# One core, third layer: where the gelus of a sequence stand, and who places the activation-table loads

## The reference, cut to what matters

```python
# attention branch: two "forgetting" attentions (forward and backward), 16 heads
f = jax.nn.log_sigmoid(xn @ Wf.T + bf)        # abs, exp and log on ACT
probs = softmax(scores + cumulated gates)     # exp on ACT
o @ Wo.T
# feed-forward branch: two small transformer layers (DEPTH = 2)
for l in range(2):
    ...local attention over windows of 64, 8 heads, softmax (exp on ACT)
    h = (h - mu) / sqrt(var + 1e-05) * lg + lb
    h = h @ w1 + b1
    a, g = jnp.split(h, 2, axis=-1)
    h = a * jax.nn.gelu(g, approximate=False)  # gelu on ACT
    x = x + h @ w2 + b2
```

## Time and profile before

| | |
|---|---|
| time, median of 3 runs | 2943.32 us (2940.13 to 2945.33) |
| profiled execution: span, first to last instruction | 2847.3 us |
| median of the runs less that span | 96.0 us |
| third layer within the span | about 665 to 2243 us |
| mean granted TensorE clock over the span | 0.954 |

### The profile page before, as it was taken

The page is one execution under the profiler, slowest core; times in us unless marked ns, Lnnn a source line. Parts: engine busy times, 40 slices in busy tenths (PEclk is TensorE's granted clock), DMA queues, the critical chain, the costliest instruction groups (busy, mean ns, idle before and its releaser), DMA issues. The chain is left out here.

```text
span 2847.3 us, 76648 instructions
## 1 busy us (share of the span) xinstructions
PE 2442.7 (86%) x30232; PEld 1812.5 (64%) x30232; DVE 2005.6 (70%) x5914; ACT 1823.8 (64%) x3779; POOL 787.6 (28%) x820
## 2 busy tenths in 40 slices
PE   6858999996889999999999899989996658999964
PEld 6745677774556666566656665666664547999943
DVE  5556544444568776877687677877775498999988
ACT  3334555553566666666666667666763488999997
POOL 3325100002133232323232223222222163111167
PEclk9959999997999999999999999999999689999998
DMA  6201355551000000000000000000000014666611
GB/s 211 38 16 40 115 158 160 155 156 56 11 17 15 4 17 17 15 4 17 17 15 4 17 17 17 9 10 13 14 13 7 1 45 156 203 195 202 192 42 51
DMA packets 104306, 175.17 MB, mean 62 GB/s; under 512 B 16273, under 2 KB 73745, under 8 KB 103825
## 3 DMA queue, kind: packets, MB, share of 16 engines
q1 hardware_dynamic: 94608, 153.20, 18.0%
q0 software_dynamic: 8192, 16.79, 2.0%
q10 hardware_dynamic: 1152, 0.27, 0.0%
HBM read 130.50 MB, written 26.74 MB: 55 GB/s over the span
## 5 line engine op out<-in xcount | busy, mean ns | idle before, releaser
L2014 POOL TENSOR_TENSOR l_rinv<-l_ssm,w_neg_half 128x8 f32<-128x8 f32 x128 | 210.2, 1642 | 551.8 <-DVE l_ssm L2305 551.7
L257 PE MATMUL bank<-l_kT,l_qT 32*128 32x128 f32 (+1 forms) x3072 | 355.0, 350 | 8.8 <-DVE l_qm L1382 7.2
L257 PE MATMUL bank<-l_qm,l_kT 32*128 32x128 f32 (+1 forms) x3072 | 350.7, 347 | 6.3 <-DVE l_qm L2215 6.3
L2045 ACT ACTIVATE l_probsT<-bank 128x768 f32<-128x768 f32 x256 | 208.5, 815 | 160.1 <-PE bank L257 159.3
L276 DVE TENSOR_REDUCE l_tops<-bank 128x2 f32<-128x256 f32 (+1 forms) x384 | 196.1, 511 | 119.9 <-PE bank L257 116.5
L2717 DVE RECIPROCAL l_rden<-l_den 128x256 f32<-128x256 f32 x128 | 223.8, 1748 | 30.0 <-ACT l_den L2628 29.4
L893 POOL DMA_INDIRECT back<-sorted_y,pos x128 | 125.6, 981 | 378.7 <-DMA sorted_y<-l_y_tile 347.8
L277 DVE TENSOR_REDUCE l_tops<-bank 128x2 f32<-128x512 f32 (+1 forms) x384 | 227.5, 592 | 0.0
L257 PEld LDWEIGHTS bank<-l_kT,l_qT 32*128 32x128 f32 x3072 | 205.8, 190 | 18.2 <-DVE l_qm L1382 9.3
L257 PEld LDWEIGHTS bank<-l_qm,l_kT 32*128 32x128 f32 x3072 | 202.9, 188 | 8.2 <-DVE l_qm L2215 8.1
L154 POOL TENSOR_TENSOR l_rstd<-l_var,w_neg_half 128x2 f32<-128x2 f32 (+1 forms) x56 | 42.6, 760 | 569.6 <-DVE l_var L149 556.8
(11 more groups left out here) (350 smaller groups left out, 6967.4 us busy)
## 6 DMA issues: line engine op xcount, KB each, us to landing
l_expert<-in_experts SPq DMA_DIRECT2D x72, 768.0 KB, 4.1
l_expert<-in_experts SPq DMA_DIRECT2D x72, 578.0 KB, 3.5
l_x_tile<-sorted_x SPq DMA_DIRECT2D x144, 64.0 KB, 4.1
sorted_y<-l_y_tile SPq DMA_DIRECT2D x144, 64.0 KB, 3.7
l_v_half<-l_v SPq DMA_DIRECT2D x32, 264.0 KB, 3.2
sorted_x<-x_all SPq DMA_DIRECT2D x18, 256.0 KB, 3.9
l_v_half<-l_v SPq DMA_DIRECT2D x32, 132.0 KB, 3.2
l_x<-in_x SPq DMA_DIRECT2D x8, 256.0 KB, 5.0
```

Source lines behind the costliest of these rows:

```text
L257: lasts.append(pe.matmul(bank[:, at:at + n * P], lhs[:, c * P:(c + 1) * P], rhs[:, x0 * P:(x0 + n) * P], start=False, stop=(i == 1), skip_ ...
L2014: pool.tensor_tensor(rinv[:, i, :], ssm[:, i, :], g.neg_half[:, 0:LH], ALU.pow).then_inc(rinv_ready[l], 1)
L2045: Bt.took(act.activation(probsT[:, (j // 2) % 2, 2 * (j % 2):2 * (j % 2) + 2, :], two[:, :, 0:AW], ACT.Exp), rd, use)
```

## The change

The three `up` items of each small layer now stand at one step (5 for small layer 0, 8 for small layer 1), and the source places the table loads: `natural_log_exp_and_others` once at the start of the third layer on ACT, `gelu_and_others` ahead of a small layer's first gelu, and `natural_log_exp_and_others` again behind its third. The order within the steps changes on every engine, since all walk `BESIDE`. No DMA is added, removed or moved.

```diff
-    3: [("o", 1, 0), ("o", 1, 1), ("qk", 0, 1), ("up", 0, 0)],
+    3: [("o", 1, 0), ("o", 1, 1), ("qk", 0, 1)],
     4: [("qk", 0, 2), ("out", 1)],
-    5: [("up", 0, 1), ("up", 0, 2)],
+    5: [("up", 0, 0), ("up", 0, 1), ("up", 0, 2)],
     6: [("shift", 1), ("down", 0), ("apply", 1)],
     7: [("normed", 1), ("qk", 0, 3)],
-    8: [("qk_t", 0, 0), ("up", 1, 0), ("up", 1, 1)],
-    9: [("up", 1, 2), ("qk_t", 0, 1)],
+    8: [("qk_t", 0, 0), ("up", 1, 0), ("up", 1, 1), ("up", 1, 2)],
+    9: [("qk_t", 0, 1)],
     10: [("down", 1), ("qk_t", 0, 2), ("hand", 1)],
...
             act.wait_ge(setup_done, 1)
+            act.preload_act_table_set("natural_log_exp_and_others")
...
                         l, m = of
+                        if m == 0:
+                            act.preload_act_table_set("gelu_and_others")
                         b = G.read(act, rd, item)
                         act.activation(gg[:, m, :], b[:, S:2 * S], ACT.Gelu,
                                        bias=w["bup2"][:, l, 1, m:m + 1]).then_inc(gelu_ready[l], 1)
+                        if m == FC - 1:
+                            act.preload_act_table_set("natural_log_exp_and_others")
```

## The result

The changed kernel takes 2917.7 us (median of 4 runs, 2913.7 to 2919.9) against 2941.7 (2938.3 to 2945.3): ratio 0.9921, 95% interval 0.9907 to 0.9936. (Ratios stand here as they were recorded with the runs; they are not exactly the quotients of the medians.) It is 24 us faster; the forecast was 15 us slower, and the time lies under both ranges, 2946 to 2970 and 2930 to 2975.

What follows compares the result with a forecast made beforehand. No engine is full; DVE sets the pace in steps 3 to 14, ACT in 16 to 18. Step 5 +16.5, steps 8 and 9 +17.5, gates -18.0, ends -1.5: +14.5 us, 2957.8 us; range 2946 to 2970, 8 in 10 2930 to 2975.

Steps and rivals of the forecast that it cites:

- What lies around the span, 96.0 us against the median of the runs, stays: Whole kernel: 96.0 us of run time outside the profiled span of 2847.3 us was taken as unaffected by the change.
- The gates: Steps 16 to 18: log and exp share a set, two loads go; 1.2 us gained a round, bounds 0.64 and 2.57.
- Step 5: Small layer 0: the third `up` waits for a bank, so DVE is 1.1 us late a round; bounds 0 and 1.9.
- The chain of 2.34: Step 5: gelu, DVE multiply, PE's pairs, gelu; 2.34 us from first gelu to third at full clock.
- Step 8: Steps 8 and 9, small layer 1: the third `up` waits for DVE; 1.25 us lost a round, bounds 0 and 1.5.
- three small differences of terms near 1 us decide: Warning on the round's sum, 1.1 + 1.25 - 1.2: if the gates give over 2.3, the kernel is not slower.
- What a load costs: ACT's table loads: the trace shows 1.30 us from load to next instruction, the Trainium skill about 2.66 for a switch.
- Faster: the batch pays: Rival, 14%: the third `up`'s bank wait is hidden at steps 5 and 8, the gates' gain stands; -19.5 us, 2924 us.
- No change: Rival, 18%: gates give 2.57 a round, or the losses at steps 5 and 8 are half as large; 2937 or 2941 us.
- Slower still: Rival, 12%: gates give only the first two waits and PE's 1.5 us carries in full; 2970 or 2982 us.
- the build would place loads of its own: Rival, 2%: the build adds its loads beside the source's, 65 more on ACT; about 2995 us.

Runs made afterwards that it cites:

- quick chip: Kind of chip (1 and 15) on which the unchanged kernel before takes 2852 to 2854 us; the changed kernel's ratio there is 1.0006.
- late profiles: Profiles on the kind of chip (14, 10, 0) where the kernel before takes 2943 to 2947 us; the changed kernel's ratios there are 0.9908 and 0.9921.
- chip 14: One of three chips where the unchanged kernel before takes 2943 to 2947 us; its profiled round there is 96.17 us.

## Why the prediction was wrong

**The step that failed** is "What lies around the span, 96.0 us against the median of the runs, stays". I took the trace for the runs' own execution. It was not: 1.7 to 3.2 us lie around a span, and the 93 us that remained were lost inside the kernel, on the kind of chip that was timed. Some of them could be won by the change. The sum had no term for PE's late signals and none for the clock, since the trace that it was read from showed neither. The table of a round makes the sum. The late signal is the rounds at full clock (94.65 before, 94.30 after) less the quick chip's; the falls are what is left of the mean over 13 rounds. The changed kernel has two late profiles:

| us a round | before | changed | difference |
|---|---|---|---|
| quick chip | 93.4 | 93.8 | +0.4 |
| late signal at step 19 | +1.2 | +0.5 | -0.7 |
| clock falls | +1.5 | +0.1, +0.35 | -1.4, -1.2 |
| late chip, mean | 96.17 | 94.42, 94.64 | -1.75, -1.53 |

Thirteen rounds give -20 to -23 us of the -24 measured. On chip 14, from the gates of the first sequence to those of the last, the kernel before took 1405.0 us and the changed one 1382.3: -22.7, nearly all in these 13 rounds. In the result's own profile the same stretch took 1380.4; there the two rounds ahead of the 13 were 4.7 us shorter as well, and differences of that size in these two rounds come and go between late profiles.

**Terms.** The gates: forecast -1.2, measured -1.47, within the bounds of 0.64 and 2.57. Step 5: forecast +1.1, measured +0.67. The chain of 2.34 was right (2.35), but on the quick kind the first gelu came 1.26 earlier in the round and not 0.8, so the last product was 0.70 late. Step 8: forecast +1.25, measured +1.03 on the late kind and 1.09 on the quick one, with the wait of 1.5 as worked out. In sum +0.34 in place of +1.15: three errors of 0.2 to 0.4, all on one side. On the quick kind the forecast's +14.5 us on the span was +5.4 (2847.7 to 2853.1), and the ratio says no change. So even there the sign was hardly to be told; "three small differences of terms near 1 us decide" was the right warning.

**What a load costs.** The 1.30 from load to next instruction held (1389.29 to 1390.59 after). The Trainium skill's 2.66 for a switch (ScalarE: Activation LUTs, What ACT_TABLE_LOAD costs) is not what these traces show.

**The rivals.** *Faster: the batch pays* named the right side for a reason that was not it: PE's bank waits were there, 0.61 and 1.51. *No change* is what the quick kind shows, with gates and losses both between its values and mine. *Slower still* had the gates at 0.64, and they gave 1.47. That the build would place loads of its own did not happen: there are 65. The Trainium skill's rule to batch calls by set (ScalarE: Activation LUTs, Table sets: the hidden batching unit) did harm where it moved gelus (+1.81 a round), and good where log and exp came to share a set (-1.47).

**Why the falls go.** The kernel before waits 0.49, 0.98 and 1.94 for ACT or behind it within 10 us; the changed one 0.56 and 1.28. Of these the last counts most: with 0.56 and 1.33 the clock fell in 3 rounds of 13, and with 0.56 and 1.90, in the same kernel on the same chip but for the added load, in 9. That the last wait shrank from 1.94 to 1.28 has a cause of its own. On a late chip PE's signals come back about 2.8 us after the gather's start: 1449.70 to 1452.48 before, 1432.66 to 1435.52 after:

```profile
1432.66 1.03 POOL L893 DMA_INDIRECT back<-sorted_y,pos  x1 [0.16 <-issue]
...
1435.52 0.18 DVE L2208 RECIPROCAL l_rrow<-bank 128x4 f32<-128x4 f32 x1 [2.41 <-PE bank L1863]
```

Before, PE began the matmuls in question 0.32 after the gather's start (1450.02), in the changed kernel 1.07 after (1433.73): with the gates' loads gone, DVE and POOL come further ahead of PE than before, and less of the held time is left. (In each of the six late profiles with the program's loads and the gather in its place, it starts 10.3 us after the gates' exponential in place of 12.5, 2.2 earlier, while PE's step 20 would be 1.5 earlier, as on the quick kind: 13.4 in place of 14.8.) That this distance sets the wait is argued from the traces and not shown; no run varied that distance in small steps.

**What stays open.** Why the chips differ, and whether a chip keeps its kind: the runs show that the signals are late on late chips when this gather falls on step 19, not what holds them. What decides between equal rounds with and without a fall. And the 46 to 59 us that late chips lose before the first gates and behind the last ones, with whatever kernel, were not studied.

## What to carry to other kernels

Hold a trace against the runs first: if span and time differ by more than a few us, the trace is of another situation, and the missing time may be what a change wins or loses. Where TensorE's clock falls behind a wait of 1 to 2 us, a microsecond taken out of that wait is worth more than itself; look for matmuls of one line with two durations. Be wary of standing three items in a row that each hold one of two banks until a long read is over: here that cost 1.81 us a round, and the four table loads saved did not pay for it.

## What the runs showed of the hardware

- The same program took 2852 to 2854 us on two chips and 2943 to 2947 on three others, each met once. On the latter, signals of PE reached ACT and DVE over 1 us late while POOL issued an indirect gather at step 19. Issuing that gather 11.4 us earlier gained 1.1% there and nothing on the others.
- On late chips TensorE's clock went from 2.4 to 1.2 GHz for 3 to 7 us behind waits of 0.49, 0.98 and 1.9 us, none over 2 us, in 9 or 10 rounds of 13; with 0.56 and 1.9 in 9; with 0.56 and 1.3 in 1 to 3; with 0.49, 0.98 and 0.73 in none.
- `natural_log_exp_and_others` served exp and log without a second load; all 65 loads took 1283 ns.
